# Narrow column strips for the matmuls of row maxima in three 16-head attentions

## What is computed

```python
q = jnp.einsum('bsd,hde->bhse', x, wq) + bq
k = jnp.einsum('bsd,hde->bhse', x, wk) + bk
v = jnp.einsum('bsd,hde->bhse', x, wv) + bv
scale = 1.0 / jnp.sqrt(jnp.asarray(q.shape[-1], q.dtype))
scores = jax.nn.softmax(jnp.einsum('bhse,bhte->bhst', q, k) * scale, axis=-1)
att = jnp.einsum('bhst,bhte->bhse', scores, v)
```

## Time and profile before

| | us |
|---|---|
| median of three runs | 4535.02 |
| lowest and highest of them | 4525.23 and 4536.65 |
| profiled execution | 4532.62 |
| its span | 4530.8 |
| PE busy | 3780.4 (83%), 32085 matmuls |
| weight loads busy | 1740.2 (38%) |
| DVE busy | 3080.0 (68%) |
| ACT busy | 2519.0 (56%) |

### The profile page before, as it was taken

The page is one execution under the profiler, slowest core; times in us unless marked ns, Lnnn a source line. Parts: engine busy times, 40 slices in busy tenths (PEclk is TensorE's granted clock), DMA queues, the critical chain, the costliest instruction groups (busy, mean ns, idle before and its releaser), DMA issues. The chain is left out here.

```text
span 4530.8 us, 85564 instructions
## 1 busy us (share of the span) xinstructions
PE 3780.4 (83%) x32085; PEld 1740.2 (38%) x32085; DVE 3080.0 (68%) x4734; ACT 2519.0 (56%) x5060; POOL 1229.4 (27%) x1200
## 2 busy tenths in 40 slices
PE   4769997650899999887999997788994889999958
PEld 4623334630333333332222223355663722222227
DVE  5467774459666666657999994434995389999833
ACT  3436665461244444433888886334542448888844
POOL 2510000510288888100000000034892500000015
PEclk7979998775899999886999998888996879999979
DMA  3221110200000000002000000120001220000012
GB/s 116 70 75 39 39 40 23 74 28 0 9 3 3 6 3 3 17 1 69 21 30 30 30 21 3 43 72 23 1 1 53 62 69 30 30 30 26 17 54 69
DMA packets 79528, 151.15 MB, mean 33 GB/s; under 512 B 20247, under 2 KB 45967, under 8 KB 78479
## 3 DMA queue, kind: packets, MB, share of 16 engines
q1 hardware_dynamic: 60579, 106.98, 7.2%
q0 software_dynamic: 13408, 24.81, 1.8%
q10 hardware_dynamic: 5132, 13.88, 0.9%
HBM read 104.08 MB, written 31.20 MB: 30 GB/s over the span
## 5 line engine op out<-in xcount | busy, mean ns | idle before, releaser
L1486 DVE TENSOR_REDUCE 33_heads_mx<-33_heads_mps 128x1 f32<-128x1024 f32 x512 | 602.6, 1219 | 47.8 <-PE 33_heads_mps L1336 45.5
L1486 DVE TENSOR_REDUCE 56_heads_mx<-56_heads_mps 128x1 f32<-128x1024 f32 x512 | 602.6, 1219 | 46.8 <-PE 56_heads_mps L1336 44.4
L1456 ACT ACTIVATE 33_heads_p<-33_heads_sps 128x512 f32<-128x512 f32 x1024 | 553.6, 596 | 86.5 <-PE 33_heads_sps L1362 83.3
L1456 ACT ACTIVATE 56_heads_p<-56_heads_sps 128x512 f32<-128x512 f32 x1024 | 553.6, 596 | 86.0 <-PE 56_heads_sps L1362 82.5
L2496 ACT ACTIVATE 22_latent_heads_p<-22_latent_heads_ring 128x512 f32<-128x512 f32 x512 | 277.4, 595 | 358.8 <-PE 22_latent_heads_ring L2415 358.8
L1486 DVE TENSOR_REDUCE 7_heads_mx<-7_heads_mps 128x1 f32<-128x1024 f32 (+7 forms) x384 | 333.7, 908 | 146.5 <-PE 7_heads_mps L1344 98.7
L2519 DVE TENSOR_REDUCE 22_latent_heads_mx<-22_latent_heads_ring 128x1 f32<-128x512 f32 x512 | 323.0, 683 | 145.5 <-PE 22_latent_heads_ring L2394 145.5
L1456 ACT ACTIVATE 7_heads_p<-7_heads_sps 128x512 f32<-128x512 f32 (+3 forms) x640 | 308.1, 533 | 154.9 <-PE 7_heads_sps L1365 114.8
L1362 PE MATMUL 33_heads_sps<-31_head_rows_qs,31_head_rows_ks 123*32 123x512 bf16 x4096 | 314.4, 383 | 8.3 <-ACT 33_heads_p L1456 5.0
L1362 PE MATMUL 56_heads_sps<-52_head_rows_qs,52_head_rows_ks 123*32 123x512 bf16 x4096 | 314.2, 383 | 8.2 <-ACT 56_heads_p L1456 5.0
L2411 PE MATMUL 22_latent_heads_ring<-22_latent_heads_qc,18_mla_mem_keys 64*128 64x512 f32 x1024 | 272.0, 608 | 3.4 <-DMA 19_mla_loop_mem_mrow<-22_latent_heads_mT 3.4
(11 more groups left out here) (1261 smaller groups left out, 6965.6 us busy)
## 6 DMA issues: line engine op xcount, KB each, us to landing
39_hale_masks_qs<-scratch_q_parts SPq DMA_DIRECT2D x45, 96.0 KB
39_hale_masks_ks<-scratch_k_parts SPq DMA_DIRECT2D x45, 96.0 KB
3_routed_experts<-in_L0f_experts SPq DMA_DIRECT2D x8, 514.0 KB
9_routed_experts<-in_L0f_experts SPq DMA_DIRECT2D x8, 514.0 KB
51_routed_experts<-in_L3f_experts SPq DMA_DIRECT2D x8, 514.0 KB
58_routed_experts<-in_L3f_experts SPq DMA_DIRECT2D x8, 514.0 KB
yT<-scratch_results SPq DMA_DIRECT2D x12, 256.0 KB, 4.5
y<-scratch_results SPq DMA_DIRECT2D x12, 256.0 KB, 4.8
```

The costliest lines, as they stand in the source:

```text
L1456: act.activation(pslot[x % PS][:, 0:CW - off], sps[e % SB][:, 0:CW - off], ACT.Exp, scale=SCALE / 2).then_inc(ex_done, 1)
L1486: dve.tensor_reduce(mx[h % 2][:, i, half:half + 1], mps[x % 2][:, 0:w], AX.X, ALU.max).then_inc(mx_taken, 1)
```

## The change

Each matmul of maxima becomes four of 32 queries, on the four column strips, in the same half of the rows as before. The mask of a diagonal unit becomes four matmuls of 32 queries over all rows. All other instructions and their order are as they were, and each semaphore is raised once per unit, by its last matmul.

```diff
                             low = HIGH if b and h else 0
-                            ins = pe.matmul(mps[x % 2][:, b:b + n], qs[h % SETS][low:low + SIX, tile(i)],
-                                            ks[h % SETS][low:low + SIX, 1024 * half + b:1024 * half + b + n],
-                                            start=True, stop=not (diag and b + n == w))
+                            for strip in range(0, P, QUAD):
+                                ins = pe.matmul(mps[x % 2][strip:strip + QUAD, b:b + n],
+                                                qs[h % SETS][low:low + SIX, P * i + strip:P * i + strip + QUAD],
+                                                ks[h % SETS][low:low + SIX, 1024 * half + b:1024 * half + b + n],
+                                                start=True, stop=not (diag and b + n == w), tile_position=(low, strip))
                         if not diag:
                             ins.then_inc(mx_ready, 1)
                     for x in xs:
                         _i, _half, w, diag = units[x % U]
                         if diag:
-                            pe.matmul(mps[x % 2][:, w - P:w], g.ident_bf[:], g.mask_q[:], start=False, stop=True).then_inc(mx_ready, 1)
+                            for strip in range(0, P, QUAD):
+                                ins = pe.matmul(mps[x % 2][strip:strip + QUAD, w - P:w], g.ident_bf[:, strip:strip + QUAD], g.mask_q[:],
+                                                start=False, stop=True, tile_position=(0, strip))
+                            ins.then_inc(mx_ready, 1)
```

## The result

| | us |
|---|---|
| before, median of 7 runs | 4528.14 (4525.23 to 4536.77) |
| changed, median of 7 runs | 4549.81 (4543.49 to 4553.14) |
| ratio | 1.0043, 95% interval 1.0032 to 1.0054 |
| profiled execution | 4550.9, its span 4549.1 |

The change makes the kernel slower, by 0.43%: 14 to 24 us by the interval. The forecast was 6 us slower, less than the 13.6 us that I had called measurable, and I had given 0.51 to no measurable change and 0.31 to slower. It came out slower, inside the stated range of 4455 to 4562 and at the upper end of the forecast's own (4525 to 4550). The loss is two to four times the forecast, so a term was sized wrongly.

A forecast was written before the change was run, and what follows sets the result against it. The plain loop's 5.01 us period was taken as bound by DVE's reductions and PE's matmuls in turn, including two edges. Late starts +9.4 and +4.2, mask edges -7.5 gave +6.1 on 4532.6: 4539 us, range 4455 to 4562.

The forecast's parts named there:

- Edges at the maxima: Both kinds of loop: every PE pause of 0.10 us between maxima and scores, masks or products stays, so 0 change.
- Rival A: Edges of the maxima: shared columns are enough to need no pause; total -68 us, 4464 us; chance 0.17.
- Edges from masks to scores: Causal loop: this pause goes; five of nine edges per head count, 0.10 us each over 15 heads, -7.5 us.
- Eight matmuls where there were two: Units of maxima: the last matmul starts 0.02 us later per burst or waited-for unit; +9.4 us plain, +4.2 us causal.
- rival C: Each pack starts slowly, at the products' 7 ns pace throughout, 0.045 us per late start; +23 us, 4556 us; chance 0.19.
- Rival B: Units of maxima: the two row halves no longer run together; +148 us, 4681 us; chance 0.08.
- Masks at no cost: Causal masks: strips run side by side, no longer than before, 0 us; their late start is counted with the burst.
- instructions covered: Plain loop on PE: 80 instructions per period at 28 ns need 2.2 of 5.01 us, so issue does not set the pace.

## Why the prediction was right or wrong

**Edges at the maxima: right.** Taken as staying in full, from the row in which rows alone differ. They stayed: 0.31 to 0.32 into the maxima. Rival A, that shared columns are enough, falls with that. The mask edge vanished in the causal loop when rows and columns both matched, so it is not that no edge can be removed.

**Edges from masks to scores: right.** I had 5 x 0.10 = 0.50 us per causal head; the masks alone bring 0.47, with their own later release in it. That exactly five of the nine edges count was not tested by itself.

**Eight matmuls where there were two: the step that failed.** The mechanism was right and its place too (the last matmul of two units per period), but the price, "+0.02 us per burst or waited-for unit", was only the later *start* on PE. It measured 20 ns. What DVE waits for is the release, and that comes 31 ns later still: a term that the forecast put at nothing without a reason. In the plain loop the step from the first unit of the pair to DVE grew by 20 + 31 = 51 ns, the one from the waiting load to the scores by 17, and the period by 64. Over 118 periods in two stages that is 0.064 x 236 = 15.1 us where I had 9.4; by the stages' lengths it is 17.7. I had given 0.045 us per late start as an upper bound and charged it to a slower issue pace (rival C). C's total, 23.2 us slower, is nearer to the medians' difference of 21.7 than the forecast's 6.1, but by luck: the starts spread over 23 ns, not over 0.05 us. That the measured time lies in the stated range says little, since the range was wide enough for three different mechanisms. In the causal loop the term was 14 x 0.02 = 0.28 us per head and measured 0.20, so there it was too large. With masks the head came to -0.27 where the forecast's terms give -0.22.

The trace of the kernel before could have told it. Nothing in the groups that I printed shows the time from a last matmul to its signal, but the semaphore events do: in the plain loop the signal of two tiles of maxima comes 405 or, off an edge, 180 ns after the last start, that of the four tiles of scores 419 or 192 ns.

The Trainium skill has a rule for this on the page that I had used for the starts (TensorE: Matmul & The Clock Gate, Part 3, The cost: per-tile semaphore tail): behind the span of a pack comes a tail that grows by about 4.7 ns for each tile. Six more tiles are 28 ns by it, and the trace says 31. As an estimate from that page's figure, the release of one unit per plain period costs 118 x 2 x 0.028 = 6.6 us more, and the forecast would have been +12.7 us.

**Rival B: wrong.** Row halves and narrow strips stream side by side: two units take 0.56 us, and all eight matmuls of one start within 23 ns.

**Masks at no cost, instructions covered: nearly right.** Four tiles release 15 ns later than one, and 16 of 24 units end on a mask; the forecast had 0 for that. The 17,660 additional loads and matmuls left no longer wait for issue in the rows above.

**The total.** Forecast +6.1 us, measured by the ratio +14 to +24. The explained part is smaller than that: 15.1 us in the plain and filtered loops less 15 x 0.27 = 4.0 in the causal one are 11.1, where the forecast had 6.1 for the same terms. The three stages account for 13.8 of the profile's 18.3; the 2.7 between lie at the ends of the loops and ahead of them, and the last 4.5 in stages that the change leaves alone. For these two parts I have no cause beyond the spread between profiles.

## What to carry to other kernels

Before splitting a matmul into strips, ask what tiling its neighbours have in rows *and* in columns. If both then match, each change of tiling saved is worth 0.10 us here where it lies on the path; if only one does, nothing is saved. Either way every tile more costs about 3.3 ns at the start and 5.2 ns at the release. Where another engine waits for the result, price the release at that engine's start, not at the matmul's.

## What the runs showed of the hardware

- Changing the tiling costs 93 to 113 ns at the full clock, whether rows, columns or both change; some 130 changes of columns alone (masks to scores) and as many of rows alone (maxima to masks) in the causal loop of the kernel before had medians of 97 and 95 ns. Where rows and columns both match, as from the narrow masks to the scores, there is no pause.
- A pack of tiles is released 5.2 ns later for each further tile (428, 438 and 459 ns from the last start to DVE for two, four and eight of 32 columns), whatever their order. The delay is in the semaphore's raise (405, 415 and 435 ns) and not in the matmul records.
- A weight load of 64 columns takes 103 ns in the records, of 32 columns 89, of 128 columns 92. A strip of 64 is the dearest choice per tile behind a change of tiling: 14 ns more at the release than with either (442 against 428 ns with two tiles).
